# Edge pass and attention of a graph network: operands of VectorE partly in PSUM, attention's VectorE order pipelined

## The reference

```python
out_i = act(jnp.concatenate([x_i, edge_attr], -1) @ W).reshape(-1, HEADS, DIM)
out_j = act(jnp.concatenate([x_j, edge_attr], -1) @ W).reshape(-1, HEADS, DIM)
alpha = act((jnp.concatenate([out_i, out_j], -1) * att).sum(-1))
...
alpha = segment_softmax(alpha, i, N_NODES)
msg = out_j * alpha[:, :, None]
aggr = jax.ops.segment_sum(msg, i, num_segments=N_NODES)
out = aggr.mean(1) + bias
```

## Time and profile before

| | us |
|---|---|
| median of 3 runs | 17995.49 (17975.62 to 18011.02) |
| the profiled execution, its own time | 17987.27 |
| its span, first to last instruction | 17985.7 |
| edge pass, 450 to 7733 | 7283 |
| attention, 8454 to 10882 | 2428 |

### The profile page before, as it was taken

One profiled execution on the slowest core, in us unless ns is written; L12 is line 12 of the kernel. 1 busy time (PEld: TensorE's weight loads), 2 busy tenths in 40 slices (PEclk: granted clock), 3 DMA queues, 4 the chain that ended last, 5 costly groups with the idle time before them and its releaser, 6 DMA issues. The chain is left out here.

```text
span 17985.7 us, 163600 instructions
## 1 busy us (share of the span) xinstructions
PE 7475.0 (42%) x27414; PEld 5058.4 (28%) x27414; DVE 6442.6 (36%) x14846; ACT 6018.5 (33%) x12123; POOL 8053.9 (45%) x8196
## 2 busy tenths in 40 slices
PE   4554444445454444500111551772333343333357
PEld 3332222323232222300101551232222232222223
DVE  5555555555555555543112772011111121111111
ACT  0344444444444444410112661013333333333310
POOL 0444444444444444447775005116666636666600
PEclk9777777777777777755555665885555565555578
DMA  1333333333333323360111551651111131111136
GB/s 24 89 97 93 98 92 97 94 97 93 96 97 93 99 93 97 94 31 25 37 32 54 183 181 43 242 202 22 22 22 22 22 102 22 22 22 22 22 132 223
DMA packets 1037233, 1461.80 MB, mean 81 GB/s; under 512 B 518414, under 2 KB 733934, under 8 KB 1011937
## 3 DMA queue, kind: packets, MB, share of 16 engines
q1 hardware_dynamic: 651986, 1075.95, 19.0%
q0 software_dynamic: 284800, 382.51, 8.7%
q10 hardware_dynamic: 100368, 2.41, 0.7%
HBM read 946.06 MB, written 512.36 MB: 81 GB/s over the span
## 5 line engine op out<-in xcount | busy, mean ns | idle before, releaser
L1554 POOL DMA_INDIRECT l2s_got<-rel_d,l2s_idx x3232 | 3073.2, 951 | 2679.9 <-POOLq L1551 1739.3
L800 POOL DMA_INDIRECT rows_d<-edge_rows,edge_place x1624 | 1679.1, 1034 | 3528.8 <-POOLq L798 3078.5
L1580 PE MATMUL l2s_ps<-l2s_got,l2s_oh 128*128 128x65 f32 (+1 forms) x6464 | 1473.2, 421 | 3399.8 <-PEq L1578 2805.6
L1580 PEld LDWEIGHTS l2s_ps<-l2s_got,l2s_oh 128*128 128x128 f32 x6464 | 1408.9, 330 | 3465.3 <-issue 3465.3
L899 PE MATMUL edge_z<-edge_w,edge_feats 128*128 128x512 f32 x3232 | 2044.4, 719 | 555.3 <-PEq L896 551.5
L1252 DVE TENSOR_TENSOR net_acc<-net_acc,l2s_ps 128x65 f32 (+1 forms) x3232 | 719.4, 223 | 4143.1 <-issue 3693.3
L913 PE MATMUL edge_at<-edge_upto,edge_oh_loT 128*128 128x50 f32 x3232 | 718.8, 310 | 3075.7 <-PEq L912 1490.6
L1270 POOL DMA_INDIRECT count_d<-all_list_val,all_list_idx x1568 | 1680.0, 1071 | 568.4 <-issue 474.7
L792 POOL DMA_INDIRECT edge_gath<-h_d,edge_idx x1624 | 1545.8, 952 | 501.2 <-issue 494.6
L971 DVE SCALAR_TENSOR_TENSOR edge_prod<-edge_soft,edge_z 128x512 f32<-128x512 f32 x808 | 552.2, 683 | 3303.1 <-DVEq L970 2966.5
L1383 PE MATMUL at_ps<-at_msg,at_oh 128*128 128x128 f32 x3520 | 761.1, 404 | 1951.8 <-PEq L1379 978.8
(11 more groups left out here) (370 smaller groups left out, 11788.2 us busy)
## 6 DMA issues: line engine op xcount, KB each, us to landing
at_rows<-rows_d SPq DMA_DIRECT2D x444, 528.0 KB
count_d<-edge_zero SPq DMA_DIRECT2D x202, 994.0 KB
l1s_cnt<-count_d SPq DMA_DIRECT2D x49, 1600.0 KB, 6.4
l3s_cnt<-count_d SPq DMA_DIRECT2D x49, 1600.0 KB, 6.4
rel_d<-l2t_out SPq DMA_DIRECT2D x100, 768.0 KB, 3.2
l1s_cnt<-count_d SPq DMA_DIRECT2D x49, 1536.0 KB, 6.1
l3s_cnt<-count_d SPq DMA_DIRECT2D x49, 1536.0 KB, 6.1
edge_drow<-loc_d SPq DMA_DIRECT2D x203, 256.0 KB
```

The source lines that it names most:

```text
L800: pool.indirect_dma_start(out=net.rows_d, out_offset=bass.IndirectOffsetOnAxis(ap=place[q][:, j:j + 1], axis=0), in_=rows[q][:, j, :], in_ ...
L1554: pool.indirect_dma_start(out=got[r][:, j, 0:cols], out_offset=None, in_=table, in_offset=bass.IndirectOffsetOnAxis(ap=idx[i][:, k:k + 1], ...
L1580: ins = pe.matmul(ps[q][:, j, 0:wide], oh[q][:, j, :], got[r][:, j, 0:wide], start=True, stop=True)
```

## The change

In the edge pass, DVE copies the attention vector to PSUM once (`att_ps`), and L978 and L982 read it there. In attention, the weights of a step are copied to PSUM by ACT (`keep_weights`, two buffers, with a semaphore `wts_kept` to DVE and `wts_free` back); the weights' DMAs get semaphores of their own (`wts_loaded`). `keep_weights` of step i + 2 stands in ACT's order between the list copies and the one-hots of step i + 1, and two of them stand ahead of the loop. DVE multiplies heads 0 and 1 into `wtd` in SBUF and heads 2 and 3 into `wtd_ps` in PSUM, in halves of 4 tiles, and makes the message from one of each, also in halves. The placement (`place`) of step i + 2 moves in between the two additions to `acc` of step i; the wait for the second addition and the release of PE's buffer move into the weighing of the next step. The block numbers are read ahead of the wait for PE.

```diff
+    att_ps = e.ps("att_ps", [P, 2, OUTJ])
...
-                v.tensor_tensor(prod[:, :, 0:OUTJ], prod[:, :, 0:OUTJ], att[:, 0:1, :].to_broadcast([P, 2, OUTJ]),
+                v.tensor_tensor(prod[:, :, 0:OUTJ], prod[:, :, 0:OUTJ], att_ps[:, 0:1, :].to_broadcast([P, 2, OUTJ]),
                                 ALU.mult)
                 v.wait_ge(out_j_made, 1).then_inc(out_j_made, -1)
                 v.sem_inc(z_free, 1)
                 v.tensor_tensor(prod[:, :, OUTJ:WIDE], rows[q][:, tiles, 0:OUTJ],
-                                att[:, 1:2, :].to_broadcast([P, 2, OUTJ]), ALU.mult).then_inc(multiplied, 1)
+                                att_ps[:, 1:2, :].to_broadcast([P, 2, OUTJ]), ALU.mult).then_inc(multiplied, 1)
...
+            v.tensor_copy(att_ps[:, :, :], att[:, :, :]).then_inc(att_kept, 1)
+            v.wait_ge(att_kept, 1)
...
-        wtd = [t.sb(f"wtd{q}", [P, G, OUTJ]) for q in TWO]
+        wtd = [t.sb(f"wtd{q}", [P, G, 2 * D]) for q in TWO]
+        wtd_ps = [t.ps(f"wtd_ps{q}", [P, G, 2 * D]) for q in TWO]
+        wts_ps = [t.ps(f"wts_ps{q}", [P, GS, SPAN, HEADS]) for q in TWO]
...
+        wts_loaded = [sem(f"wts_loaded{r}") for r in range(4)]
...
+                def keep_weights(r):
+                    s.wait_ge(wts_loaded[r], 16 * GS).then_inc(wts_loaded[r], -16 * GS)
+                    s.wait_ge(wts_free, 1).then_inc(wts_free, -1)
+                    s.copy(wts_ps[r % 2][:, :, :, :], wts[r][:, :, :, :]).then_inc(wts_kept, 1)
+
                 s.sem_inc(til_free, 4)
                 s.sem_inc(blk_free, 2)
+                s.sem_inc(wts_free, 2)
                 for r in TWO:
                     list_tiles(r * GS, r)
+                for r in TWO:
+                    keep_weights(r)
                 one_hots(0)
                 with Loop(nc, s, GROUPS) as it:
                     for r in range(4):
@@ -1340,6 +1356,7 @@
                         list_tiles(w0 + 2 * GS, (r + 2) % 4)
                         s.wait_ge(blk_free, 1).then_inc(blk_free, -1)
                         s.copy(blk[r % 2][:, :], net.row_bsrc[:, bass.ds(w0, GS)]).then_inc(blk_listed, 1)
+                        keep_weights((r + 2) % 4)
                         one_hots(1 - r % 2)
...
-                            for out, items in ((rows, row_items), (wts, weight_items)):
+                            for out, items, landed in ((rows, row_items, loaded), (wts, weight_items, wts_loaded)):
                                 item = items[bass.ds(starts[j], 1), :, :, :].rearrange("n p t r -> (n p) t r")
-                                sp.dma_start(out[r][:, j, :, :], item).then_inc(loaded[r], 16)
+                                sp.dma_start(out[r][:, j, :, :], item).then_inc(landed[r], 16)
                     free_values(nc, starts)
                     sp.sem_inc(til_free, 1)
 
@@ -1362,7 +1379,6 @@
                 with Loop(nc, sp, GROUPS):
                     for r in range(4):
                         fetch((r + 2) % 4)
-                sp.wait_ge(loaded[1], 32 * GS)
 
             @block.gpsimd
             def _(pool):
@@ -1370,7 +1386,7 @@
 
             @block.tensor
             def _(pe):
-                pe.sem_inc(ps_free, 2)
+                pe.sem_inc(ps_free, 1)
...
-                def prepare(w0, q, r):
-                    v.wait_ge(loaded[r], 32 * GS).then_inc(loaded[r], -32 * GS)
+                def place(w0, q, r):
+                    v.wait_ge(loaded[r], 16 * GS).then_inc(loaded[r], -16 * GS)
                     v.tensor_tensor(
                         loc[q][:, :].rearrange("p (g t) -> p g t", t=SPAN),
                         net.bsrc[:, bass.ds(w0, GS)].unsqueeze(2).to_broadcast([P, GS, SPAN]),
                         rows[r][:, :, :, OUTJ + HEADS], ALU.subtract).then_inc(placed, 1)
+
+                def weigh(q, r, n, added_before=False):
+                    tiles = slice(n, n + SPAN)
                     rq = rows[r][:, :, :, :].rearrange("p g t r -> p (g t) r")
-                    wq = wts[r][:, :, :, :].rearrange("p g t h -> p (g t) h").unsqueeze(3)
-                    for n in range(0, G, 2):
-                        ins = v.tensor_tensor(
-                            wtd[q][:, n:n + 2, :].rearrange("p g (h d) -> p g h d", h=HEADS),
-                            rq[:, n:n + 2, 0:OUTJ].rearrange("p g (h d) -> p g h d", h=HEADS),
-                            wq[:, n:n + 2, :, :].to_broadcast([P, 2, HEADS, D]), ALU.mult)
-                    ins.then_inc(weighted, 1)
-                    v.wait_ge(weighted, 1).then_inc(weighted, -1)
+                    wq = wts_ps[q][:, :, :, :].rearrange("p g t h -> p (g t) h").unsqueeze(3)
+                    v.tensor_tensor(
+                        wtd[q][:, tiles, :].rearrange("p g (h d) -> p g h d", h=2),
+                        rq[:, tiles, 0:2 * D].rearrange("p g (h d) -> p g h d", h=2),
+                        wq[:, tiles, 0:2, :].to_broadcast([P, SPAN, 2, D]), ALU.mult)
+                    if added_before:
+                        v.wait_ge(added, 1).then_inc(added, -1)
+                        v.sem_inc(ps_free, 1)
+                    return v.tensor_tensor(
+                        wtd_ps[q][:, tiles, :].rearrange("p g (h d) -> p g h d", h=2),
+                        rq[:, tiles, 2 * D:4 * D].rearrange("p g (h d) -> p g h d", h=2),
+                        wq[:, tiles, 2:4, :].to_broadcast([P, SPAN, 2, D]), ALU.mult)
+
+                def messages(q, n):
+                    tiles = slice(n, n + SPAN)
+                    return v.tensor_tensor(msg[q][:, tiles, :], wtd[q][:, tiles, :], wtd_ps[q][:, tiles, :], ALU.add)
+
+                def prepare(q, r, added_before):
+                    v.wait_ge(wts_kept, 1).then_inc(wts_kept, -1)
+                    weigh(q, r, 0, added_before).then_inc(weighted_first, 1)
+                    weigh(q, r, SPAN).then_inc(weighted_last, 1)
+                    v.wait_ge(weighted_first, 1).then_inc(weighted_first, -1)
+                    messages(q, 0)
+                    v.wait_ge(weighted_last, 1).then_inc(weighted_last, -1)
                     v.sem_inc(rows_free, 1)
-                    v.tensor_tensor(msg[q][:, :, :], wtd[q][:, :, 0:2 * D], wtd[q][:, :, 2 * D:4 * D],
-                                    ALU.add).then_inc(messaged, 1)
+                    v.sem_inc(wts_free, 1)
+                    messages(q, SPAN).then_inc(messaged, 1)
 
                 done = net.v_done.of(v)
                 done(v.memset(acc[:, :], 0.0))
-                prepare(0, 0, 0)
+                v.sem_inc(added, 1)
+                place(0, 0, 0)
+                prepare(0, 0, False)
+                place(GS, 1, 1)
                 with Loop(nc, v, GROUPS) as it:
                     for r in range(4):
                         q = r % 2
                         w0 = (it * 4 + r) * GS
-                        prepare(w0 + GS, 1 - q, (r + 1) % 4)
+                        prepare(1 - q, (r + 1) % 4, True)
                         v.wait_ge(blk_listed, 1).then_inc(blk_listed, -1)
+                        blocks = item_values(nc, v, blk[q], NBU * P)
+                        v.sem_inc(blk_free, 1)
                         v.wait_ge(summed, 1).then_inc(summed, -1)
-                        add_items(net, v, acc, blk[q], added, lambda j: ps[q][:, j, :], 2 * D)
-                        v.sem_inc(ps_free, 1)
-                        v.sem_inc(blk_free, 1)
+                        with Scratch(nc, v):
+                            here = acc[:, bass.ds(blocks[0], 2 * D)]
+                            v.tensor_tensor(here, here, ps[q][:, 0, :], ALU.add).then_inc(added, 1)
+                        place(w0 + 2 * GS, q, (r + 2) % 4)
+                        v.wait_ge(added, 1).then_inc(added, -1)
+                        with Scratch(nc, v):
+                            here = acc[:, bass.ds(blocks[1], 2 * D)]
+                            v.tensor_tensor(here, here, ps[q][:, 1, :], ALU.add).then_inc(added, 1)
+                        free_values(nc, blocks)
+                v.wait_ge(added, 1)
```

## The result

The changed kernel takes 19162.40 us (median of 4 runs, 19155.26 to 19185.68), the kernel before beside it 17993.15 us (4 runs, 17975.62 to 18011.02). The ratio is 1.0652, with a 95% interval of 1.0634 to 1.067: slower by 1169 us, 207 us more than the forecast of 18955 and inside its range. One thing must be known to read the experiments. The kernel before took 17993 us here and 18267 us in the first series of experiments, but 13407 and 13419 us in the two later ones, in which signals between engines did not arrive late beside GpSimd's indirect DMAs. Two runs of the first prompt series, one of 18755 us of the kernel before and one of 13742 us, had a lower granted clock than the others of their kernel and stand in no ratio.

The account below looks back on a forecast made before the run. Late signals beside GpSimd's DMA issue were taken to bound the edge pass and attention beside the scatter; free steps took 6.07 us. 17987 + 943 (attention, ACT's serial cycle) + 25 (edge pass) = 18955 us, range 18650 to 19260.

Parts of the forecast that it names:

- The serial cycle of ACT: Attention: ACT waits each step for a fetch issued on its own list copy; step 11.0 us against 6.07, +943, chance 0.82.
- Today this is covered: nobody on ACT waits for it: Free attention before the change: the 6.6 to 7.1 us from list copy to landing delays nobody on ACT.
- Steps beside the scatter: Attention during GpSimd's count scatter: 36 steps fit in its 1336 us, bounds 31 and 41, against 41 before.
- The rival of two lists a step: Attention beside the scatter: fetch signal and landing each cost a list's rest, about 20 steps; 19131 us, chance 0.05.
- The rival that the weights land in time: Attention: ACT's wait costs nothing, DVE's saved stalls bring the step to about 5.0 us; 17694 us, chance 0.08.
- The edge pass: Attention vector in PSUM for L978 and L982: +25 us, bounds -100 (GpSimd's relief passes through) and +150 (groups lengthen).
- I take the middle: Edge pass: +25 us chosen between -100 and +150, the latter from two groups differing by 0.75 us.

Follow-up runs that it names:

- behind the one-hots: Changed kernel with keep_weights moved after the one-hots in ACT's loop; 18834.02 us, ratio 1.0306 to the kernel before.
- the copy one step later: Changed kernel with ACT copying the weights of step i + 1 instead of i + 2; 18446.79 us, ratio 1.0095 to the kernel before.
- the attention part alone: Changed kernel with the edge pass reading the attention vector in SBUF again; 19196.05 us, ratio 1.0508 to the kernel before.
- the edge part alone: Kernel before with only L978 and L982 reading att_ps in PSUM; 18477.43 us, ratio 1.0117 with late signals; 13413.75 us, 0.9994 with prompt ones.
- the faster kernel: Kernel before with the changed attention, weights copied for step i + 1, edge pass as before; 13300.92 us, ratio 0.9915, prompt signals.
- The two pauses: Edge operands in PSUM plus GpSimd memset and wait after each group's second and fifth scatter; 13407.92 and 13423.45 us, ratios 1.0001 and 1.0004, prompt signals.

## Why the prediction was right, and which term was mis-sized

**The serial cycle of ACT (+943 forecast).** Right in mechanism and size. Attention took 3377 us instead of 2428, +949. The step of 11.0 us was 11.09; its parts, 6.6 to 7.1 to the landing with 0.3 for the copy and 3.52 for the one-hots, were 7.17 and 3.65 in the timeline. It is shown by taking it away twice: behind the one-hots the cycle loses 3.2 us, most of the one-hots' time; one step later two steps share it, and the step is 5.88.

**"Today this is covered: nobody on ACT waits for it."** This reading was wrong, and nothing in the sum rested on it. The earlier trace rows show ACT idle 1.84 us at 10008.01, until L1325, the wait for DVE's placement; the placement itself waits for the landing. Group and timeline of the kernel before:

```profile
L1327 ACT ACTIVATE at_far<-all_iota,at_loc 128x128 f32<-128x128 f32 x1440 | 440.5, 388 | 374.2 <-ACTq L1325 374.2
```

```profile
10013.86 2.45 ACT L1327 ACTIVATE at_far<-all_iota,at_loc 128x128 f32<-128x128 f32 x8 [2.06 <-ACTq L1325]
```

From list copy to the placement of the same step it is 7.86 us, to ACT's squares 0.29, and to the list copy of two steps later 3.88, the mean over 148 free steps, in each of which both engines waited: 12.04 us for two steps, the 6.02 of a free step. So the kernel before ran on the same chain, spread over two steps. The change drew it together into one, and the copy one step later spread it out again.

**Steps beside the scatter (36 forecast of 31 to 41).** 37, and 36 in the attention part alone. The rival of two lists a step did not occur.

**The rival that the weights land in time.** Ruled out by the 6.88 us of idling with either kind of signals. Its other half, that DVE's saved stalls bring the step to 5.0, was not borne out: with the chain over two steps again the step was 5.88 with late signals, and 1311 / 221 = 5.93 with prompt ones. DVE's stalls of the earlier trace rows were mostly the fetch's lateness, 214 of 257 us before the placement, which a new order on DVE does not remove.

**The edge pass (+25 forecast, bounds -100 and +150).** This is the mis-sized term: +255 in the profiles, +210 as the edge part alone, and both lie outside its bounds. That the whole time still fell into the range is slack elsewhere: the range allowed attention +1112, and it took +949. The parts of this term held: DVE's own time did not move (678 against 682 ns), GpSimd's scatters fell to 981 ns against a forecast of near 970.

"I take the middle" failed. The middle had no row in its favour, and the one pair of groups that was compared, 0.75 us of lengthening, was taken as the far end, though the groups of before already differed by more: the 5th and the 95th of a hundred lie at 35.4 and 36.7 us. They differed by when ACT's second exponential came: within 17 us of the first scatter in 116 of 198 groups, which took 35.5 us, and after 20 us or more in 17, which took 36.7. After the change it came within 17 us in 28 groups and after 20 or more in 169, at 35.4 and 37.4 us. The mean group was 1.26 us longer, and the second exponential came 5.5 us later, of which some 1.3 reach the end of the group.

That the edge operands cause it is shown by the kernel that has them alone, and that it needs late signals by the same kernel at 0.9994 with prompt ones. How a GpSimd that issues 0.3 us faster makes a signal 5 us later is not settled; the pauses made to test it never met late signals.

**The sum.** 949 + 255 is 1204, less 6 in stages that the change does not touch, is the 1198 between the two profiled spans.

## What to carry to other kernels

A copy that is put in an in-order engine's loop makes that engine wait for whatever feeds the copy: follow the source back, and where it leads to something the same engine has just made, the whole way there and back stands in every step, however many buffers the ring has. Taking the item one step older shared it between two steps; copying the lists further ahead might share it among more, and was not tried. When an engine seems to be free of such a chain, look at what ended its idle time: here it waited through another engine. Read who bounds a stage before paying for relief of an engine: operands in PSUM came with a gain of 118 us in attention, where GpSimd ended the stage last, and with none in the edge pass, where it did not. Where engines wait for signals beside another engine's DMA issue, freeing that engine can cost; bound such a term by the spread of the groups that are there, not by the middle of two.

## What the runs showed of the hardware

**One kernel, two behaviours.** The kernel before took 17993 and 18267 us in two series and 13407 and 13419 in two others. With late signals an edge group takes 35.8 us, its second exponential comes 15.9 us after the first scatter, and a step of attention beside the scatter takes 32.6. With prompt ones the edge group of the faster kernel, whose edge pass is that of before, takes 21.96 us and its second exponential comes after 6.0; a step of attention, as before and with the scatter beside it throughout, takes 1339 / 221 = 6.06 in the kernel with the edge part alone. The difference is seen at SP too: a DMA issue beside the count scatter, first of the changed kernel with late signals, then of the faster kernel with prompt ones, both from the timeline:

```profile
9186.13 0.70 SPq L1372 DMA_DIRECT2D at_rows<-rows_d  x1
```

```profile
6102.98 0.33 SPq L1368 DMA_DIRECT2D at_rows<-rows_d  x1
```

0.70 against 0.33 us; free of the scatter it is 0.33 with late signals as well. The series of 18267 us and that of 13407 us ran on the same chip, so the chip alone does not set it. What does was not found.

**Two SBUF operands hold GpSimd's DMA issue up.** An indirect DMA of the count lists takes 0.97 us alone and up to 1.50 beside a weighting with both operands in SBUF; with `wts_ps` in PSUM the mean falls from 1152 to 1053 ns, 156 us over 1568. The Trainium skill, SBUF — State Buffer, section Who interferes with whom, says that such an instruction contends with a GpSimd instruction that reads SBUF, through the shared read interface. The traces agree for GpSimd's indirect DMAs, with 1.50 us against 0.97.

**Relief that reaches nobody.** In the edge pass with prompt signals the operands in PSUM shortened GpSimd's part of a group from 20.93 to 20.06 us, and its waiting grew from 1.03 to 1.90: the group took 21.96 us without them and 21.92 and 21.97 with them. GpSimd looked like the bound there, waiting only 1 us after its last gather, and was not alone: another chain of about the same length stood beside it. The two pauses say the same, as they lengthened GpSimd's part by 1.5 us and the group by nothing. Which chain that is was not followed.
